# Wavelet stage: the restoring product of the kernel as three single-pass products of rounded parts, one step later

## What is computed

```python
x = x + _L0_conv_ref(_ln_c(x), s_ll, s_lh, s_hl, s_hh, w1, b1, w2, b2)

# _ln_c: (v - mean over channels) / sqrt(var over channels + 1e-6)
def _L0_conv_ref(x, ...):
    ll, lh, hl, hh = haar_dwt(x)                 # 2x2 pixels -> four half-size bands
    ll = ll * exp(s_ll) ...                      # each band scaled per channel
    low_proj = einsum('bchw,oc->bohw', concat([ll, lh, hl, hh], 1), w1) + b1
    restored = einsum('bchw,oc->bohw', low_proj, w2) + b2
    return haar_idwt(*split(restored, 4))        # back to full size
```

## Time and profile before

| | us |
|---|---|
| median of 3 runs | 2119.15 (2116.65 to 2120.28) |
| the profiled execution, device time | 2120.05 |
| its span in the trace | 2118.2 |
| wavelet stage | about 14 to 329 of the span |
| expert choice behind it | about 330 to 450 |
| busy share over the span: PE, PEld, DVE, ACT, POOL | 95%, 72%, 56%, 47%, 24% |
| idle of POOL before L533, ended by DVE's L568 | 133.2, over 64 chunks |

### The profile page before, as it was taken

One profiled execution on the slowest core, in us unless ns is written; L12 is line 12 of the kernel. 1 busy time (PEld: TensorE's weight loads), 2 busy tenths in 40 slices (PEclk: granted clock), 3 DMA queues, 4 the chain that ended last, 5 costly groups with the idle time before them and its releaser, 6 DMA issues. The chain is left out here.

```text
span 2118.2 us, 41606 instructions
## 1 busy us (share of the span) xinstructions
PE 2006.2 (95%) x14926; PEld 1535.6 (72%) x14926; DVE 1189.5 (56%) x2548; ACT 1005.5 (47%) x2815; POOL 511.4 (24%) x622
## 2 busy tenths in 40 slices
PE   6999993599999989999999999999999799999998
PEld 3555551367777779999999999999999544444443
DVE  4777777756666652222222222232222399999998
ACT  4666664343434423333344444444444555555552
POOL 4555553222222210000000000000000455555552
PEclk9999996599999999999999999999999799999999
DMA  3955551132222200000000000000000256666653
GB/s 110 243 166 164 165 156 54 56 100 85 96 95 86 100 31 12 0 0 0 0 4 0 0 0 0 12 9 0 0 0 0 79 151 158 159 155 163 159 147 90
DMA packets 192676, 159.10 MB, mean 75 GB/s; under 512 B 25848, under 2 KB 159000, under 8 KB 192536
## 3 DMA queue, kind: packets, MB, share of 16 engines
q1 hardware_dynamic: 190840, 156.89, 26.4%
q0 software_dynamic: 512, 0.53, 0.1%
q10 hardware_dynamic: 1184, 0.00, 0.0%
HBM read 56.70 MB, written 67.11 MB: 58 GB/s over the span
## 5 line engine op out<-in xcount | busy, mean ns | idle before, releaser
L1208 PE MATMUL s_ps<-g_ring,g_T 128*128 128x128 f32 x7620 | 855.7, 274 | 8.5 <-DVE g_ring L1255 8.5
L1208 PEld LDWEIGHTS s_ps<-g_ring,g_T 128*128 128x128 f32 x7620 | 854.6, 191 | 9.2 <-DVE g_ring L1255 9.1
L1244 DVE SCALAR_TENSOR_TENSOR g_ring<-s_ps,s_xs 128x128 f32<-128x128 f32 x508 | 148.4, 292 | 418.6 <-PE s_ps L1208 418.6
L1307 ACT ACTIVATE g_X<-g_ring 128x256 f32<-128x256 f32 x254 | 172.4, 679 | 295.9 <-DVE g_ring L1244 295.9
L1687 DVE TENSOR_TENSOR tm_Z<-tm_pg,tm_nd 128x1024 f32<-128x1024 f32 x256 | 301.7, 1210 | 7.5 <-PE tm_pg L1527 6.3
L1541 PE MATMUL tm_po<-tm_Z,g_wexp 128*64 128x512 f32 x1024 | 249.3, 608 | 0.0
L1291 ACT ACTIVATE g_X<-g_ring 64x256 f32 x256 | 106.8, 417 | 205.6 <-DVE g_ring L1244 203.3
L1244 DVE SCALAR_TENSOR_TENSOR g_ring<-s_ps,g_X 128x128 f32<-128x128 f32 x254 | 74.0, 291 | 211.1 <-PE s_ps L1208 211.1
L1623 POOL TENSOR_TENSOR g_X<-g_x,g_X 128x512 f32<-128x512 f32 x64 | 82.9, 1297 | 349.4 <-POOLq L1184 286.0
L1302 ACT ACTIVATE s_xs<-g_X 128x256 f32<-128x256 f32 x254 | 161.3, 636 | 0.6 <-PEq L1184 0.6
L1541 PEld LDWEIGHTS tm_po<-tm_Z,g_wexp 128*64 128x64 f32 x1024 | 62.5, 137 | 109.8 <-issue 107.9
(11 more groups left out here) (273 smaller groups left out, 2879.5 us busy)
## 6 DMA issues: line engine op xcount, KB each, us to landing
tm_nd<-g_X SPq DMA_DIRECT2D x256, 128.0 KB, 2.4
g_X<-in_x SPq DMA_DIRECT2D x128, 128.0 KB, 2.9
x1s<-g_X SPq DMA_DIRECT2D x64, 256.0 KB, 2.1
x1tok<-g_X SPq DMA_DIRECT2D x64, 256.0 KB, 2.5
g_x<-x2s SPq DMA_DIRECT2D x64, 256.0 KB, 2.9
y<-tm_yo SPq DMA_DIRECT2D x128, 128.0 KB, 2.5
g_X<-x1s SPq DMA_DIRECT2D x32, 256.0 KB, 2.8
x2s<-g_X SPq DMA_DIRECT2D x32, 256.0 KB, 2.0
```

Source lines behind the costliest of these rows:

```text
L1208: last = pe.matmul(out, g.T[i][:, d * P:d * P + P], g.ring[(u - 1) % RING][:, images(c), d:d + 64], start=(d == 0), stop=(d == ND - 1))
L1244: dve.scalar_tensor_tensor(g.ring[n % RING][:, images(c), inner], conv, 0.0, x[:, images(c)], ALU.max, ALU.add).then_inc(y_ready[c], 1)
L1307: act.activation(line(*place(n)), g.ring[n % RING][:, :, inner], ACT.Copy).then_inc(stored, 1)
```

## The change

restore's two fp32 products become six of one pass each. `lowH` is low rounded to fp32r, `lowL` the remainder, `BH` and `BL` the same for `g.Brec`; the sum of BL x lowH, BH x lowH and BH x lowL is made for each of the two halves. To have the parts, ScalarE reads `tv` twice (into `lowS` and into `lowH`), GpSimd subtracts (`low_of_low`, last in its step), and VectorE makes BH and BL once at the start. restore(c-3) now stands directly behind centre(c), where restore(c-2) stood at the end of the step; and VectorE does high_of_square(c) ahead of add_restored(c-3).

```diff
@@ tensor
-                pe.wait_ge(exact_ready, 1)
+                pe.wait_ge(exact_ready, 3)
                 def restore(c):
                     wait(pe, s["low_s"], c + 1)
+                    wait(pe, s["low_l"], c + 1)
                     wait(pe, s["x1"], c)
                     for v in range(2):
-                        last = pe.matmul(rec[:, v * (N // 2):(v + 1) * (N // 2)], g.Brec[:, v], lowS[c % 2],
-                                         start=True, stop=True)
+                        out = rec[:, v * (N // 2):(v + 1) * (N // 2)]
+                        pe.matmul(out, BL[:, v], lowH[c % 2], start=True, stop=False)
+                        pe.matmul(out, BH[:, v], lowH[c % 2], start=False, stop=False)
+                        last = pe.matmul(out, BH[:, v], lowL[c % 2], start=False, stop=True)
                     last.then_inc(s["rec"], 1)
@@ scalar, copy_low
                     wait(act, s["low"], c + 1)
+                    wait(act, s["low_l"], c - 1)
+                    act.activation(lowS[c % 2], tv[:, 0:N // 2], ACT.Identity, bias=g.b1[:])
                     wait(act, s["rec"], c - 1)
-                    act.activation(lowS[c % 2], tv[:, 0:N // 2], ACT.Identity, bias=g.b1[:]).then_inc(s["low_s"], 1)
+                    act.activation(lowH[c % 2], tv[:, 0:N // 2], ACT.Identity, bias=g.b1[:]).then_inc(s["low_s"], 1)
@@ gpsimd
+                def low_of_low(c):
+                    wait(pool, s["low_s"], c + 1)
+                    wait(pool, s["rec"], c - 1)
+                    pool.tensor_tensor(lowL[c % 2], lowS[c % 2], lowH[c % 2].bitcast(F32), ALU.subtract
+                                       ).then_inc(s["low_l"], 1)
@@ vector
                 dve.tensor_copy(Cmr[:], g.Cm[:]).then_inc(exact_ready, 1)
+                dve.tensor_copy(BH, g.Brec).then_inc(exact_ready, 1)
+                dve.wait_ge(exact_ready, 2)
+                dve.tensor_tensor(BL, g.Brec, BH.bitcast(F32), ALU.subtract).then_inc(exact_ready, 1)
```

More of the change, by code:

```diff
@@ L336, in wavelet_mixer @@
         s = {n: m.sem(n) for n in (
-            "centred", "squared", "var", "lnv", "rstd", "normed", "low", "low_s", "rec", "x1",
+            "centred", "squared", "var", "lnv", "rstd", "normed", "low", "low_s", "low_l", "rec", "x1",
             "high", "parts", "xhigh", "xparts", "tcentred", "tsquared", "tturned", "tcopied", "logits", "tvar",
@@ L345, in wavelet_mixer @@
         xr, sq, rr, nn, lowS, tsq, ts, trs = g.xr, g.sq, g.rr, g.nn, g.lowS, g.tsq, g.ts, g.trs
+        lowH, lowL = ([m.sb(f"{n}{i}", [P, N // 2], F32R)[:] for i in range(2)] for n in ("lowH", "lowL"))
+        BH, BL = (m.sb(n, [P, 2, P], F32R)[:] for n in ("BH", "BL"))
         tok_dst = g.x1tok.rearrange("b j w x -> b w j x")
@@ L464, in _ @@
                         centre(c)
+                    if now(c - 3):
+                        restore(c - 3)
                     if now(c - 1):
@@ L474, in _ @@
                         turn(c - 3)
-                    if now(c - 2):
-                        restore(c - 2)
             @block.scalar
@@ L546, in _ @@
                         low_of_x(c + 2)
+                    if now(c - 2):
+                        low_of_low(c - 2)
             @block.vector
@@ L595, in _ @@
                 for c in range(CHUNKS + LAG + 1):
+                    if now(c):
+                        high_of_square(c)
                     if now(c - 3):
                         add_restored(c - 3)
-                    if now(c):
-                        high_of_square(c)
                     if now(c + 2):
```

## The result

The changed kernel takes 2184.36 us (median, 2183.26 to 2186.09); beside it the kernel before took 2119.72. The ratio is 1.0307, with a 95% interval of 1.0289 to 1.0325: 3.1% slower. The forecast was 2169.5 with a range of 2149 to 2184; the direction came out, and so did the chain of waits in the main; the size missed the range by 0.4 us, for one cost that the chain had wrong. The profiled execution took 2185.43 us, 65.4 more than the one of before.

The account below looks back on a forecast made before the run. TensorE's queue bounded the wavelet stage; the move's chain of waits would take a pair of steps from 9.54 to 11.09 us. 2120.05 + 49.6 + 0.7 = 2170.4, less 0.9 to the median, gave 2169.5 us, range 2149 to 2184.

Parts of the forecast that it names:

- The three releases named ahead: VectorE's L586 released by variance; TensorE idle before L448 in plain steps until L579, before L441 until ScalarE's L508.
- The product: restore on TensorE: six one-pass products take 0.73 us in place of 0.86, its queue 0.13 shorter in each step.
- the rounding of x 0.34: VectorE's path to normalise in the plain step: 0.34 us from the rounding of x to the next instruction's start.
- 5.79 forecast: Plain step, from centre's start through variance, rounding and GpSimd's remainders to restore of the gate step: 5.79 us.
- 5.30 forecast: Gate step, restore to the next plain step: restore could start at 5.79 us, the next plain step at 11.09.
- both hide behind GpSimd's remainder: Plain step: token_centre's wait for x1 and normalise's path let centre end at 5.19 us, before lowL's 5.79.
- The start: Two 256-column VectorE instructions ahead of the first rounding of x: 0.7 us taken, at most 1.1.
- The clock: Rival: stalls drop TensorE to 1.2 GHz, its 6.2 us of chain terms double, + 198, 2368 us; chance 0.02.
- the weight loads: Rival: weight loads don't overlap, restore takes 1.15 us, 0.42 more twice a pair, + 26.9, 2196 us; chance 0.06.
- GpSimd's remainder was a limit: Forecast's view; the rival had it no limit, plain part 5.19 not 5.79, pair 10.49, 2150 us; chance 0.11.
- a TensorE that stays the bound at 2111.5: Rival: in the wavelet stage only the shorter queue counts, 9.28 us a pair, 2111.5 us; chance 0.04.
- The three ends that it names: Around the forecast: lowL -1.9 to +1.0 us, restore -0.6 to +8.3, five assumed releases -4.8 to +8.

Follow-up runs that it names:

- e7: The changed kernel with restore as two fp32 products of lowS again, its new place, waits and parts kept: 2194.09 us, ratio 1.0356 to the kernel before.
- e10: e4 with restore as two fp32 products of lowS, the parts made but not used: 2122.64 us, ratio 1.0026 to the kernel before.
- e2: The changed kernel with GpSimd's remainder of low ahead of its remainder of x: 2172.59 us, ratio 1.0255 to the kernel before.
- e4: The changed kernel with restore(c-3) at the step's end, x1's users a step later, lowH from lowS, lowL and addition first: 2111.86 us, ratio 0.9962 to before.

## Why the prediction was wrong in size and right in kind

- **Bound and place.** Right in kind. TensorE's queue was the bound, the move made it wait, and the direction of 3% came from that. The three releases named ahead are in the trace: L586 by the variance, L448 by L579 (0.77 idle, 0.8 forecast), L441 by L508 (0.17, 0.26 forecast); so is the fourth, restore by `lowL`, though the profile's label there is "issue".
- **The product.** 0.73 was taken. In the changed kernel's plain step the distances are 0.12 and the six take 201.57 - 200.86 = 0.71, but in the gate step, after a stall, the six take 207.30 - 206.51 = 0.79. e7 and e10 put the gain over fp32 at 0.15 to 0.16 a step, against 0.13.
- **The term that failed.** "the rounding of x 0.34" of VectorE's path, and `xl` straight behind `sql` in GpSimd's (1.36 from start to start, measured 1.64). Both came from the earlier trace rows, where the rounding starts 0.17 ahead of GpSimd's instruction. With the addition between, it starts 0.62 behind, and takes 0.93; from its start to the next instruction's it is 204.29 - 203.43 = 0.86, not 0.34. The rows of before held a trace of it, `sql` at 1.39, longer than `xl` at 1.28, which the prediction used as a duration without asking why.
- **The sum, term by term.** From centre in the plain step to restore in the gate step: 5.79 forecast, 206.48 - 200.39 = 6.09 measured, of which `xl` starts 0.30 late (4.06 in place of 2.40 + 1.36 = 3.76). From there to the next plain step: 5.30 forecast, 211.96 - 206.48 = 5.48 measured, 0.09 of it in low to token_variance (209.56 - 207.85 = 1.71 against 1.62) and the rest in the product. Together 0.48 x 32 = 15 us: the whole gap between 50 and 65.
- **"both hide behind GpSimd's remainder".** Only just. The next centre was forecast to start at 4.72 and started at 5.39 (L413 at 206.02, less 0.24, less 200.39), since the longer rounding stands on VectorE's path too. So 0.26 a pair is left to `lowL` by the times, 0.36 by e2, in which restore's slow start after the stall (0.79 against 0.71) goes too; not 0.60.
- **The start.** 0.7 us taken. VectorE's first instruction to the rounding of x: 0.14 before, 0.81 after (14.37 to 15.18), 0.67.
- **The rivals.** The clock held at 1.00; the weight loads overlap; GpSimd's remainder was a limit, for 0.36 of the pair. The other side, a TensorE that stays the bound at 2111.5, needed the chain to vanish. e4 makes it vanish and ends at 2111.9, by 0.31 a pair less fixed costs; the agreement to 0.4 us is in part luck.
- **The range.** The forecast's own range was 2162 to 2183. The three ends that it names add up to 2162 and 2187, so its top lies 4 short of their sum. It had ends for `lowL`, restore and the releases, but none for two engines' instructions getting longer when they come to lie side by side. One such end, the 0.11 of the earlier trace rows or more, would have carried the stated top past 2184.

## What to carry to other kernels

An instruction moved on an in-order queue changes what its neighbours overlap with: list for each moved or delayed instruction of VectorE which GpSimd instruction is running when it now starts. In these traces a rounding from SBUF to SBUF has to be priced at that one's end plus 0.28; the instructions with an input in PSUM keep their length. The cheaper form of the product was worth 0.15 a step in either place (e7, e10); what decided was the place. With the operands ready a step ahead the loop lost nothing (e10), in the chain the kernel lost 65 us. So where a product's operands need two engines more, try it and everything behind it a step later rather than forward into a chain. Where steps of two lengths alternate, sum the pair: what a wait takes in the short step can be given back in the long one, and an edit can win in one what it loses in the other.

## What the runs showed of the hardware

- A rounding fp32 to fp32r of 128x512 on VectorE, SBUF to SBUF, takes 0.42 us alone. Started 0.62 or 0.44 us into a GpSimd subtraction with two SBUF inputs, it takes 0.93 or 1.13 and ends 0.27 to 0.30 after that instruction, in all but the first few of the 64 steps of each trace. Started first, it keeps 0.42, and GpSimd's takes 1.40 in place of 1.27. In e2 the 128x256 subtraction that starts beside it takes 0.91 in place of 0.73.
- The additions L579 and normalise L591 of VectorE, with one input in PSUM, show no such lengthening: the pair of additions takes 0.87 beside GpSimd and 0.88 alone (L561), normalise 0.66 to 0.69 beside it and 0.69 alone (the last chunk of the kernel before).
- Six one-pass products of 256 columns with a weight load each run at 0.12 us apart when nothing stalls, as in the first scan, and TensorE kept its full clock through stalls of up to 0.8 us in every pair of steps.
